# A four-layer graph kernel: in its last stage GpSimd copies indices once per group instead of once per tile, and gathers into eight buffers instead of two

## The reference

```
z   = leaky_relu(lap_mul(A, x) @ W1 + b1)
d2  = sq[:, None] + sq[None, :] - 2 * (z @ z.T)
S   = exp(-sqrt(max(d2, 0) + 1e-10) / 2)
S   = where(rank of S in its row < 4, S, 0)
A2  = S + A
out = lap_mul(A2, x) @ W2 + b2       # lap_mul(A, x) = d * (A @ (d * x)), d = 1/sqrt(row sums of A)
x   = x + out
```

## Time and profile before

| | us |
|---|---|
| median of three runs (lowest, highest) | 1762.82 (1762.29, 1764.53) |
| time of the profiled execution | 1762.45 |
| its span in the trace | 1760.7 |
| PE busy | 1564.3 (89%) |
| DVE busy | 1276.0 (72%) |
| POOL busy | 575.6 (33%) |
| mean granted clock of TensorE | 0.965 of full speed |

### The profile page before, as it was taken

How to read it: one execution, slowest core, us unless ns; L and a number is a source line. 1 busy time by engine, 2 the same in 40 slices (tenths; PEclk the granted TensorE clock), 3 DMA queues, 4 the chain that set the end, 5 groups by cost and what they waited for, 6 DMA issues and landing times.

```text
span 1760.7 us, 37056 instructions
## 1 busy us (share of the span) xinstructions
PE 1564.3 (89%) x11433; PEld 1028.2 (58%) x11433; DVE 1276.0 (72%) x3508; ACT 700.5 (40%) x1113; POOL 575.6 (33%) x816
## 2 busy tenths in 40 slices
PE   3699999968888888999979999699999999889993
PEld 3467767647777777566646666578544444345552
DVE  5389999988999999455557666242599999944443
ACT  2334444425555555033332223466455555610000
POOL 2423233337777777011110001233000000047765
PEclk9999999988999999999999999899999999989997
DMA  4467777743433333222213223144100000024441
GB/s 156 174 250 262 289 271 288 286 151 90 122 113 101 113 100 116 82 96 95 93 34 125 83 88 114 55 132 125 37 1 6 6 12 6 6 91 154 152 140 48
DMA packets 97578, 205.11 MB, mean 116 GB/s; under 512 B 10912, under 2 KB 61728, under 8 KB 89328
## 3 DMA queue, kind: packets, MB, share of 16 engines
q1 hardware_dynamic: 73008, 172.58, 28.5%
q0 software_dynamic: 11840, 25.52, 5.2%
q10 hardware_dynamic: 12672, 6.29, 1.2%
HBM read 178.13 MB, written 26.21 MB: 116 GB/s over the span
## 4 chain that ended last, share of the span: by engine, by line
PE 45%; DVE 23%; issue 16%; POOL 9%; DMA 3%; ACT 2%; DVEq 1%; POOLq 1%; SPq 1%; ACTq 0%
PE bank L687 17%; PE bank L556 7%; PE bank L755 6%; DVE partsA L2063 6%; POOL gath L1385 5%; PE bank L822 4%; DVE gath L1659 3%; PE bank L641 3%; DVE cand L1526 2%; PE bank L561 2%; PE bank L541 2%; DMA gath<-last_features,idx_now 2%; PE bank L521 2%; POOL gath L1302 1%; PE bank L511 1%
## 5 line engine op out<-in xcount | busy, mean ns | idle before, releaser
L687 PE MATMUL bank<-partsB,panel 128*128 128x387 bf16 (+1 forms) x2048 | 354.5, 334 | 25.9 <-DVE agg L1460 12.1
L687 PEld LDWEIGHTS bank<-partsB,panel 128*128 128x128 fp8e4 x2048 | 202.7, 99 | 173.3 <-issue 27.1
L822 PE MATMUL bank<-wide,partsA 128*128 128x512 f32 x512 | 263.2, 596 | 6.3 <-ACT rows L1104 4.9
L641 PE MATMUL bank<-partsB,first 128*128 128x128 bf16 x3072 | 222.0, 221 | 35.6 <-DVE gath L1659 21.2
L1526 DVE MAX8 cand<-bank 128x8 f32<-128x128 f32 x1024 | 217.1, 279 | 42.1 <-POOL found L1213 21.7
L641 PEld LDWEIGHTS bank<-partsB,first 128*128 128x128 fp8e4 x3072 | 194.3, 98 | 80.7 <-issue 62.4
L556 PE MATMUL bank<-partsA,panel 128*128 128x387 bf16 x1024 | 218.1, 336 | 23.6 <-DVE cand L1526 14.3
L889 ACT ACTIVATE panel<-bank 128x1024 fp8e4<-128x1024 bf16 x128 | 130.7, 1023 | 175.9 <-PE bank L541 175.9
L1302 POOL DMA_INDIRECT gath<-pool_features,idx_now x160 | 162.9, 1018 | 55.3 <-issue 46.7
L1104 ACT COPY rows<-bank 128x512 f32<-128x512 f32 x256 | 133.3, 615 | 116.3 <-DVE partsA L2079 87.6
L1659 DVE TENSOR_REDUCE gath<-bank 128x128 f32<-128x512 f32 x256 | 172.8, 681 | 7.5 <-PE bank L641 7.1
(11 more groups left out here) (274 smaller groups left out, 2173.6 us busy)
## 6 DMA issues: line engine op xcount, KB each, us to landing
rows<-in_adj SPq DMA_DIRECT2D x64, 1024.0 KB, 7.2
panel<-adjT_panels SPq DMA_DIRECT2D x128, 512.0 KB
adjT_panels<-panel SPq DMA_DIRECT2D x32, 512.0 KB, 3.0
panel<-adjT_panels SPq DMA_DIRECT2D x64, 256.0 KB, 2.9
gath<-pool_features,idx_now POOLq DMA_INDIRECT x160
overflow_maxima<-wide POOLq DMA_DIRECT2D x1, 2048.0 KB, 19.1
pool_features<-gsc ACTq DMA_DIRECT2D x8, 256.0 KB, 2.3
rows<-overflow_maxima SPq DMA_DIRECT2D x8, 256.0 KB
```

The costliest lines, as they stand in the source:

```text
L641: i = pe.matmul(first_bank(n, peeled)[:, b * P:(b + 1) * P], first[:, q % 2, j, :], pparts[:, j, k * FE:k * FE + F], start=(k == 0), stop= ...
L687: i = pe.matmul(bank[q][:, 0:3 * w], panel[:, q, j, :], of_block if w < FE else parts_of[u][:, j, :], start=(j == 0), stop=(j == NT - 1))
L822: pe.matmul(o[:, :], zs[:, q % 2, :], zT[:, c * 512:(c + 1) * 512], start=True, stop=False)
```

## The change

Four things change, all of them in the last stage.

1. **Indices.** `stage_near` copies the 16 indices of a whole group at a time (128x16) into one of two rows of `IDX`, whose earlier contents are no longer needed. Group 0 is copied at the start; group g+1 between tiles 1 and 2 of group g. The wait for the copy's end stands ahead of the first gather of the next group, thus two tiles later.
2. **Buffers.** The gathered rows go to eight buffers `near` (two groups of four tiles) within the memory of `gath`, and each has its own semaphore. GpSimd may begin on tile t once VectorE has added tile t-8; ahead of the copy for group g+1 it waits until tile 4g-1 has been added.
3. **A new wait.** Ahead of tile t GpSimd waits until VectorE has taken t-2 products, the last one of which is that of tile t-3.
4. **Loops.** Two groups at the start and two at the end are written out, and the loop runs three times over two groups.

VectorE has the same instructions in the same order, with other buffers and semaphores. TensorE, ScalarE and SyncE are untouched.

```diff
+        near = [gath[:, i // G, (i % G) * TOP:(i % G + 1) * TOP, :] for i in range(2 * G)]
...
-            def last_gathers(g, q):
-                t = NT + g * G + q
-                pool.wait_ge(s_gath_used, t + 1)
-                pool.tensor_copy(idx_now[:, q % 2, 0:TOP], TI[:, ds(g * G + q, 1), :].rearrange("p a k -> p (a k)")
-                                 ).then_inc(s_idx, 1)
-                pool.wait_ge(s_idx, t + 1)
+            near_idx = [IDX[:, r, :] for r in range(2)]
+
+            def stage_near(g, r):
+
+                pool.tensor_copy(near_idx[r], TI[:, ds(g * G, G), :].rearrange("p q k -> p (q k)")).then_inc(s_idx, 1)
+
+            def last_gathers(g, r, q):
+                t = g * G + q
+                pool.wait_ge(s_sum, 2 * NT + t + 2)
+                if q == 0:
+                    pool.wait_ge(s_idx, NT + g + 1)
                 pool.sem_inc(waited["pool"], 1)
                 for k in range(TOP):
-                    pool.indirect_dma_start(gath[:, q % 2, k, :], None, g2_dram,
-                                            bass.IndirectOffsetOnAxis(idx_now[:, q % 2, k:k + 1], axis=0)
-                                            ).then_inc(s_gath2[q % 2], 16)
-            with pool.Fori(0, NG) as g:
-                for q in range(G):
-                    last_gathers(g, q)
+                    pool.indirect_dma_start(near[r * G + q][:, k, :], None, g2_dram,
+                                            bass.IndirectOffsetOnAxis(near_idx[r][:, q * TOP + k:q * TOP + k + 1], axis=0)
+                                            ).then_inc(s_gath2[r * G + q], 16)
+
+            def last_group(g, r, first_pair=False, last=False):
+                for q in range(G):
+                    if q == 2 and not last:
+                        if not (first_pair and r == 0):
+                            pool.wait_ge(s_gath_used, NT + g * G + 2)
+                        stage_near(g + 1, 1 - r)
+                    if not first_pair:
+                        pool.wait_ge(s_gath_used, NT + (g - 2) * G + q + 1 + 2)
+                    last_gathers(g, r, q)
+
+            stage_near(0, 0)
+            last_group(0, 0, True)
+            last_group(1, 1, True)
+            with pool.Fori(1, NG // 2 - 1) as h:
+                last_group(2 * h, 0)
+                last_group(2 * h + 1, 1)
+            last_group(NG - 2, 0)
+            last_group(NG - 1, 1, last=True)
...
-                    dve.wait_ge(s_gath2[q % 2], 16 * TOP * (g * 2 + q // 2 + 1))
+                    dve.wait_ge(s_gath2[r * G + q], 16 * TOP * (h + 1))
```

More of the change, by code:

```diff
@@ L253, in program @@
         s_gath = [sem(f"rows_gathered{i}") for i in range(2)]
-        s_gath2 = [sem(f"nearest_gathered{i}") for i in range(2)]
+        s_gath2 = [sem(f"nearest_gathered{i}") for i in range(2 * G)]
         s_gath_used = sem("gathered_used")
@@ L2097, in _, with last @@
             dve.wait_ge(s_sinv, 2 * NG)
-            def last(g, r, peeled):
+            def last(h, r, peeled):
+                g = 2 * h + r
                 c = Count(g * 16)
@@ L2107, in last @@
                     dve.wait_ge(s_sum, (g + 2 * NG) * G + q + 5)
-                    dve.wait_ge(s_gath2[q % 2], 16 * TOP * (g * 2 + q // 2 + 1))
+                    dve.wait_ge(s_gath2[r * G + q], 16 * TOP * (h + 1))
                     for k in range(TOP - 1):
-                        dve.scalar_tensor_tensor(agg[:, q, 0:F], gath[:, q % 2, k, :], sg[:, q, k:k + 1],
+                        dve.scalar_tensor_tensor(agg[:, q, 0:F], near[r * G + q][:, k, :], sg[:, q, k:k + 1],
                                                  agg[:, q, 0:F], ALU.mult, ALU.add).then_inc(s_last, 1)
                         dve.wait_ge(s_last, c.up())
-                    dve.scalar_tensor_tensor(agg[:, q, 0:F], gath[:, q % 2, TOP - 1, :], sg[:, q, TOP - 1:TOP],
+                    dve.scalar_tensor_tensor(agg[:, q, 0:F], near[r * G + q][:, TOP - 1, :], sg[:, q, TOP - 1:TOP],
                                              agg[:, q, 0:F], ALU.mult, ALU.add).then_inc(s_gath_used, 1)
@@ L2126, in _ @@
             last(0, 0, True)
-            last(1, 1, True)
+            last(0, 1, True)
             with dve.Fori(1, NG // 2) as h:
-                last(h * 2, 0, False)
-                last(h * 2 + 1, 1, False)
+                last(h, 0, False)
+                last(h, 1, False)
 _INS = ['x', 'adj', 'L0_gnn_weight', 'L0_gnn_bias', 'L1_gnn_weight', 'L2_gnn_W', 'L3_gnn_W1', 'L3_gnn_b1',
```

## The result

The changed kernel takes 1734.82 us (median of 4, 1733.34 to 1736.4), the kernel before beside it 1763.09 (4, 1762.29 to 1764.53): ratio 0.9839, 95% interval 0.9822 to 0.9856. The profiled execution took 1733.34 us, its span 1731.3.

The account below looks back on a forecast made before the run. GpSimd's pace through the last stage's gathers was taken as the limit. Savings of 17.0 + 0.5 + 3.6 + 1.7 = 22.8 us take the span from 1760.7 to 1737.9, the median to 1740.0 us; range 1736 to 1747.

Parts of the forecast that it names:

- What bounds the stage: Last stage: GpSimd's own pace through 128 gathers is the limit; TensorE's products end first, some 20 us of gathers follow.
- 24 boundaries without copy, 1.01 to 0.30: Last stage, between tiles: 24 boundaries lose copy and wait, each going from 1.01 to 0.30 us, saving 17.0 us.
- 7 boundaries with copy: Last stage, between tiles that keep a copy: 0.50 us instead of 1.01 each, saving 3.6 us.
- tile 2's wait: Last stage: with eight buffers tile 2 no longer waits for VectorE to add tile 0, saving 1.7 us.
- slow spots: Last stage: longer gathers and extra idle time between gathers, about 5 us, kept unchanged in the forecast.
- Rival A: Last stage: slow spots fall away as the loop turns 3 times, not 8; 5 us less, 1735; 9 in 100.
- the lower end of the gap behind a copy: Last stage: a gather behind a copy without a wait for it starts after 0.30 us, not 0.81.
- D: Last stage: the new wait closes a ring of GpSimd and VectorE waits; slower, 1775 us; 2 in 100.
- the new waits: Last stage: GpSimd's waits for products taken and ahead of copies cost nothing; slack nearly 10 and 7.6 us.
- VectorE's wait for gathers: Last stage: VectorE's waiting for gathered rows falls from 106.6 to about 84 us.
- TensorE without idle time and done by 1722: Last stage: TensorE has no idle time from 1575.82 us on and is done by about 1722.
- C: Last stage: TensorE becomes the limit by losing more than its 9 us in hand; 1755 us; 4 in 100.

Follow-up runs that it names:

- short sets: Runs made together on one chip in which the kernel before took about 1763 us.
- `group_copy_again`: Against the changed kernel: two buffers with the old wait for them, no wait for products, indices still copied once a group; short set, 1740.21 us, ratio 0.9877.
- `tile_copy_again`: Against the changed kernel: every tile's indices copied and waited for, no wait for products, eight buffers kept; long set, ratio 0.9998.
- `product_wait_one`: Changed kernel with its wait on products two tiles tighter (product of tile t-1 taken ahead of tile t); short set, 1753.93 us, ratio 0.995.
- experiment 3: Changed kernel with a wait for the copy's end right behind each of the seven copies; long set, 1916.1 us, ratio 1.007.
- `after_again`: The changed kernel run again, nothing altered; short set, 1734.99 us against 1762.9 for the kernel before, ratio 0.9842.
- `product_wait_two`: Changed kernel with its wait on products one tile tighter (product of tile t-2 taken ahead of tile t); short set, 1738.61 us, ratio 0.9864.
- long sets: Runs made together on one chip in which the kernel before took 1900 to 1921 us instead of 1763.
- `after_third`: The changed kernel run a third time, nothing altered; long set, 1914.11 us against 1899.9 for the kernel before, ratio 1.0081.
- `after`: The changed kernel's first measurement and profile, against the kernel before; 1734.82 us, ratio 0.9839.
- `no_product_wait_again`: Changed kernel without its wait on products taken; long set, 1964.03 us, ratio 1.0329.

## Why the prediction was off by more than its range

**What bounds the stage: right (short sets).** All 128 gathers had to come off GpSimd's queue, and their span fell by 26.1 us; the tail behind the last gather's start stayed at 9.5 us (1731.3 - 1721.8; before 1760.7 - 1751.2). The sum, term by term:

| term | forecast | measured |
|---|---|---|
| 24 boundaries without copy, 1.01 to 0.30 | 17.0 | 17.0 |
| first gather of these, 0.97 to 0.95 | 0.5 | 0.5 |
| 7 boundaries with copy | 3.6 | 4.5: 1.01 to 0.20 + 0.17 |
| tile 2's wait | 1.7 | 1.7 |
| slow spots | 0 | about 2.3 |
| first gather starts sooner | 0 | 3.3 |
| sum, on the span | 22.8 | 29.3 (the span fell by 29.4) |

Three terms were mis-sized, and all three the same way. The two of the stage itself (2.3 and 0.9 us) would have left the time inside the range: 1763.09 - 26.1 = 1737.0. What took it out, by 1.2 us, is the term that the sum didn't have, and that one is in good part chance.

**The step that failed first: "Slow spots. I keep the 5 us."** Worked out alike for both profiles (span of the gathers, less 127 steps of 1.247 or 1.246 us, the boundaries' extra and tile 2's wait), they were 5.3 us and are 3.0. Rival A, that all fall away, was half right, but its reason wasn't: in `group_copy_again` and `tile_copy_again`, which have the changed kernel's loops, tile 28's gap is there (2.09 and 1.66 us), and in neither short-set profile of the changed kernel is there a gap by "issue" over 0.31 us ahead of a gather. So the turn of the loop doesn't make it. Two gaps account for the 2.3 us: this one (2.22 instead of 0.30), and that ahead of tile 21's first gather, which in both profiles of before is 1.33 where other tiles have 0.81. What makes them stays open, as do the small delays that are left; the change of loops and copies doesn't keep tile 28's gap away for certain, since `product_wait_one`, which has both, shows 0.99 us there in a short set. (The prediction also reads TensorE's last five slices as 9, 9, 8, 9, 3; they are 8, 9, 9, 9, 3, and nothing rests on it.)

**The second: the lower end of the gap behind a copy.** I put it at 0.30, "the gap ahead of every gather that waits for nothing". That gap is one between two gathers; behind a copy it is 0.17 (7 boundaries x 0.13 = 0.9 us). The choice between the ends was right: experiment 3 shows that the 0.81 was the wait. The Trainium skill, page "GPSIMD Engine Reference", section 2.1 "Instruction dispatch", says that a completion holds back only what waits on its semaphore; 0.17 against 0.80 agrees.

**The third: a term that the sum didn't have.** The stage began 3.3 us sooner, 0.26 of it because the first copy follows the last split after 0.23 us instead of 0.49. The rest can't be told from chance: in the seven short-set profiles of the experiments the first gather starts between 1559.8 and 1566.4 us, with next to nothing changed ahead of it, and the changed kernel itself has 1559.9 in its first profile and 1564.8 in `after_again`; before it was 1563.2. A single profile can't tell such a difference from a gain, and a range of -3 and +7 us around the likeliest, made from terms of one stage only, left it out. The medians, over executions, show 28.3 us; if the stage took as long in all of them as in the profiled ones, 26.1 are of the stage and 2.2 of this kind.

**Steps that held.** Tile 2's first gather was to come 10.25 us behind the first (1573.5 - 1563.25); it came 10.20 behind. No wait of GpSimd for VectorE longer than 0.31 us: the new waits cost nothing, and D didn't occur; the gathers of `product_wait_two` (161.8 us) show that one tile tighter would have cost nothing either, `product_wait_one` that two tiles would. VectorE's wait for gathers: forecast 84, measured 79.6. TensorE without idle time and done by 1722: done at 1716.1, of which 4.5 us come from its earlier start. It has 7.7 us in hand (1731.3 against 1716.1 + 7.5), where I had said 9; by this estimate another 8 us off the gathers would meet C.

**What no rival held.** I gave 2 in 100 to slower. In the runs on record it is faster, but in long sets the changed kernel is 0.7 to 0.8% slower. C came nearest: in `after_third` TensorE's last matmul ends at 1901.8 us and the kernel 7.5 us later, just the tail that I gave TensorE. But I looked for it in waits for panels, and these stayed at 1.6 us there; the loss is in "issue" and in takes that come late. In the one profile of before there were 2.6 us of this in 300, nothing to see it by.

The Trainium skill, page "Runtime: NRT & Kernel Launch", section "Instruction fetch mechanics", says that engines fetch instructions in blocks of 16 KB by a DMA queue of their own, and that a branch out of the window forces a fetch. By this rule a TensorE so slow would fetch more often or wait for a fetch. The traces speak against both. The pages of `after` and of `after_third` count the same packets:

```profile
q8 instruction: 31, 0.51, 0.1%
q14 instruction: 28, 0.23, 0.0%
```

And in the slow stretches (1714.3 to 1741.4 us of `after_third`, 1724.3 to 1762.1 of `no_product_wait_again`) there is no packet of either queue; the next one comes within 2.4 us behind the recovery, so it can't have caused it. What did hold TensorE up no run here shows.

## What to carry to other kernels

On GpSimd, copy indices well ahead and in one piece: a copy with a wait right behind it put 1.01 us between two gathers, one whose result is needed only later 0.37, and none 0.30. When a range is made from terms of one stage, look at a second profile of the same kernel for how far the stage's start wanders; here that alone was several us. Where GpSimd's gathers are made dense, try a bound on how far they may run ahead of TensorE: here it cost nothing in short sets, and 50 us hung on it in the long one where both were run. Measure such a change more than once, beside the kernel before: here its sign depended on the set.

## What the runs showed of the hardware

- Between a copy on GpSimd and an indirect DMA that doesn't wait for it stand 0.17 us, less than the 0.30 between two indirect DMAs.
- In long sets TensorE can be held up while GpSimd gathers: in `after_third` 12 matmuls of 128x384 took 27 us, with starts 0.70 to 2.8 us apart. The granted clock fell to 0.50 of full speed (its lower level, 1.2 GHz) behind a stretch in which TensorE was busy for 0.65 of 5.70 us (1714.3 to 1720.0); at the same clock the matmuls after the recovery came every 0.33 us, and every 0.17 at 1.00. The recovery came about 5 us after the gathers stopped (4.6, 4.8 and 5.9).
- In the same sets VectorE took products up to 27 us after the record of their last matmul (1714.23 and 1741.60), and in all three profiles with a long slow stretch it did so within 0.2 us of TensorE's recovery (1741.43 and 1741.60, 1752.41 and 1752.60, 1762.10 and 1762.24).
- The same gather, tile 28's second, stood for 2.22 us in both profiles of the kernel before, in a short and a long set, and for 1.66 to 2.24 in all four with one half of the change, yet for 0.30 us in both short-set profiles of the changed kernel, which has the same gathers. In long sets the changed kernel has 1.57 in one profile and 0.30 in the other.
